# Feed forward of a transformer block: four tiles of each layer in a row, and a batch's output added two tiles later

## The reference

```
h = _layernorm(x, ln3_g, ln3_b)
p = h @ ff_w1 + ff_b1                       # 256 -> 2048
a, gate = (p[..., :D_FF], p[..., D_FF:])    # D_FF = 1024
h = a * jax.nn.gelu(gate, approximate=False) @ ff_w2 + ff_b2   # 1024 -> 256
return h + x
```

## Time and profile before

| what | value |
|---|---|
| time, median of 3 runs | 2804.77 us (2804.6 to 2804.89) |
| the profiled execution | 2804.19 us, its span 2802.4 us |
| PE / DVE / ACT / POOL busy over the span | 99% / 79% / 67% / 59% |
| TensorE's mean granted clock | 0.999 |
| feed forward, 2500 to 2600 us: PE / DVE / ACT / POOL | 100.00 / 55.82 / 42.25 / 51.14 us |
| one batch of the feed forward | 16.40 us, 144 matmuls |

### The profile page before, as it was taken

The page is one execution under the profiler, slowest core; times in us unless marked ns, Lnnn a source line. Parts: engine busy times, 40 slices in busy tenths (PEclk is TensorE's granted clock), DMA queues, the critical chain, the costliest instruction groups (busy, mean ns, idle before and its releaser), DMA issues.

```text
span 2802.4 us, 73115 instructions
## 1 busy us (share of the span) xinstructions
PE 2782.4 (99%) x25278; PEld 2488.9 (89%) x25278; DVE 2212.5 (79%) x3432; ACT 1885.2 (67%) x5979; POOL 1664.0 (59%) x1500
## 2 busy tenths in 40 slices
PE   8999999999999999999999999999999999999999
PEld 7888888888888888888888888888888899999999
DVE  7888888888888888888888888888888865555554
ACT  6776777777777777777777777777777754444443
POOL 5555555555555555776666666666666665555554
PEclk9999999999999999999999999999999999999999
DMA  6666666666666666677777777677767632222222
GB/s 160 150 162 165 162 161 158 161 156 155 150 150 153 156 157 153 152 182 177 180 181 176 177 181 170 165 169 171 172 169 168 156 101 87 75 75 85 83 75 65
DMA packets 355330, 413.34 MB, mean 147 GB/s; under 512 B 122016, under 2 KB 209440, under 8 KB 355232
## 3 DMA queue, kind: packets, MB, share of 16 engines
q1 hardware_dynamic: 345088, 395.29, 58.2%
q10 hardware_dynamic: 10144, 16.78, 1.6%
HBM read 94.52 MB, written 49.02 MB: 51 GB/s over the span
## 4 chain that ended last, share of the span: by engine, by line
PE 94%; POOL 2%; DVE 2%; issue 0%; ACT 0%; DMA 0%; SPq 0%; DVEq 0%; ACTq 0%; POOLq 0%
PE unit_ps L641 53%; PE unit_ps L666 15%; PE s_ps L653 14%; PE s_ps L641 12%; POOL probs L1385 1%; DVE blocks L1151 1%; DVE neg_max L1137 1%; POOL w_lo L1380 1%; ACT probs L936 0%; DVE qk L1163 0%; DMA pT<-blocks 0%; DVE w_lo L1097 0%; DVE hT L1132 0%; POOL x_rb L1372 0%; DMA x_ln<-in_x_dram 0%
## 5 line engine op out<-in xcount | busy, mean ns | idle before, releaser
L1385 POOL TENSOR_TENSOR probs<-probs,row_inv 128x1024 f32<-128x1024 f32 x512 | 971.5, 1897 | 827.6 <-DVE row_inv L1142 827.5
L936 ACT ACTIVATE probs<-s_ps,neg_max 128x256 f32<-128x256 f32 x2048 | 947.1, 483 | 467.9 <-DVE neg_max L1137 466.9
L1151 DVE STREAM_TRANSPOSE blocks<-probs 128x1024 f32<-128x1024 f32 x512 | 633.0, 1236 | 148.1 <-POOL probs L1385 147.5
L1137 DVE TENSOR_REDUCE neg_max<-s_ps 128x4 f32<-128x1024 f32 x512 | 612.4, 1196 | 12.7 <-PE s_ps L653 5.6
L641 PE MATMUL unit_ps<-hT_hi,w_hi 128*128 128x256 f32 x2048 | 580.0, 287 | 4.2 <-DVE hT_lo L1182 2.3
L641 PE MATMUL unit_ps<-hT_hi,w_lo 128*128 128x256 f32 x2048 | 554.9, 277 | 0.0
L641 PE MATMUL unit_ps<-hT_lo,w_hi 128*128 128x256 f32 x1792 | 497.4, 278 | 0.0
L666 PE MATMUL unit_ps<-pT,v_f 128*64 128x256 f32 x4096 | 456.4, 381 | 0.1
L936 ACT ACTIVATION_READ_ACCUMULATOR probs<-s_ps,neg_max 128x1 f32 x2048 | 437.9, 214 | 0.0
L653 PEld LDWEIGHTS s_ps<-qk 64*128 64x128 f32 x6144 | 375.2, 185 | 70.4 <-issue 53.3
L653 PE MATMUL s_ps<-qk 64*128 64x256 f32 x6144 | 427.1, 285 | 5.7 <-ACT probs L936 5.2
(11 more groups left out here) (81 smaller groups left out, 4917.3 us busy)
## 6 DMA issues: line engine op xcount, KB each, us to landing
pT<-blocks SPq DMA_DIRECT2D x1024, 256.0 KB, 4.5
rows_t_dram<-row_blocks SPq DMA_DIRECT2D x91, 256.0 KB, 2.4
rows_in<-rows_t_dram SPq DMA_DIRECT2D x91, 256.0 KB, 4.6
x_res<-in_x_dram SPq DMA_DIRECT2D x32, 256.0 KB, 3.1
x_sa_dram<-x_out SPq DMA_DIRECT2D x32, 256.0 KB, 2.2
x_ln<-x_sa_dram ACTq DMA_DIRECT2D x32, 256.0 KB, 4.4
ctx_in<-in_ctx_dram SPq DMA_DIRECT2D x32, 256.0 KB, 4.1
x_res<-x_sa_dram SPq DMA_DIRECT2D x32, 256.0 KB, 3.4
```

What stands on the lines that cost most here:

```text
L936: op = nc.scalar.activation(probs[:, m % 2, r, :].rearrange("p (j b c) -> p j b c", j=IT, c=BLK), scored.rearrange("p (j c b) -> p j b c", ...
L1137: nc.vector.tensor_reduce(neg_max[:, m % RING, :], s_ps[:, m % 2, :, :].rearrange("p h (i j) -> p (h i) j", j=S), AX_X, ALU.max, negate=Tr ...
L1151: nc.vector.transpose(blocks[:, n % 2, :, m % 2, :].rearrange("p b (j r c) -> p r j b c", j=IT, c=BLK), probs[:, m % 2, :, :].rearrange("p ...
L1385: nc.gpsimd.tensor_tensor(probs[:, m % 2, :, :], probs[:, m % 2, :, :], row_inv[:, m % RING, :].unsqueeze(2).broadcast_to([P, ROWS, S]), A ...
```

## The change

In a middle batch and in the last one TensorE now takes `hidden` 0 to 3, then the downs 4 to 7 of the batch before, then `hidden` 4 to 7, then its own downs 0 to 3. The first batch and the drain follow: the first does its downs 0 to 3 only (0 behind tile 5), the drain the downs 4 to 7. DVE adds the output of batch t-1 behind tile 3 rather than behind tile 1. Nothing is changed in the lists of ACT, POOL and SP.

```
                 if parts in (STEADY, LAST):
-                    for m in range(0, FT, 2):
+                    for m in range(FT // 2):
                         hidden(t, m, parity)
-                        hidden(t, m + 1, parity)
-                        for d in (m - 2, m - 1):
-                            if d >= 0:
-                                down(t, d)
-                            else:
-                                down(t - 1, d + FT)
+                    for m in range(FT // 2, FT):
+                        down(t - 1, m)
+                    for m in range(FT // 2, FT):
+                        hidden(t, m, parity)
+                    for m in range(FT // 2):
+                        down(t, m)
                     return
...
-                    if m < 2 and "prv" in parts:
-                        down(t - 1, m + FT - 2)
+                    if m < FT // 2 and "prv" in parts:
+                        down(t - 1, m + FT // 2)
...
-                        for d in {4: (0,), 5: (1,), 6: (2, 3), 7: (4, 5)}.get(m, ()):
+                        for d in {5: (0,), 6: (1,), 7: (2, 3)}.get(m, ()):
                             down(t, d)
...
-                    if m == 1 and "prv" in parts:
+                    if m == 3 and "prv" in parts:
                         dve.wait_ge(ff.xrb_done, t)
```

## The result

| | before | after |
|---|---|---|
| median, us | 2804.83 (2804.6 to 2806.04) | 2826.67 (2824.26 to 2827.98) |
| ratio, 95% interval | | 1.0076 [1.0064, 1.0089] |
| profiled execution; its span | 2804.19; 2802.4 | 2825.83; 2824.0 |
| busy in the span: PE, DVE, POOL | 2782.4, 2212.5, 1664.0 | 2789.8, 2188.0, 1674.4 |

A forecast was written before the change was run, and what follows sets the result against it. TensorE, busy 99% of the span, was taken as the bound. Late loads in SP's queue lengthen batches by 0.48 or 0.66 us; with batch 1 and the ends this sums to +16.45, forecast 2821 us, range 2802 to 2833.

The forecast's parts named there:

- Bound, pace: Feed forward: TensorE is full; two fewer returns from down to hidden save 0.04 us a batch, 16.36 if nothing waits.
- Cover of the addition on PE and DVE: Middle batches: addition done at 8.85 instead of 5.16, banks wanted only at 13.6, so the delay is free there.
- The chain behind it: SP's queue: store and loads move by 3.7 us, rows_lo ends late, next batch starts 0.48 (odd: 0.66) us later.
- The queue's delay: SP's queue: from the addition's end to L626 stays 2.35 us in even batches, 2.53 in odd ones.
- The sequencer's 0.45: Batch start on TensorE: 0.45 us taken between the wait for rows_lo and the first matmul; zero the other end.
- the small stall: Rival at the batch start: sequencer's 0.45 mostly hidden, 2808 us, covering 2803 to 2812 outside the forecast; chance 0.10.
- The block: POOL's remainder beside DVE's rows_lo: they exclude each other, rows_lo ends 0.54 behind it; without this, 2.7 us lower.
- Batches 1 and 2: First batches: late landings in batch 1 add 0.8 us to its odd 0.66; batch 2 loses the even 0.48.
- Start and end: Kernel's ends: returns saved in first and last two batches -0.1 us; covered wait for POOL at the end -0.65.
- The sum: Whole kernel: 16.4 for the batches, 0.8 for batch 1, -0.1 and -0.65 give +16.45 us.
- What would show it: Profile signs: PE 3 to 4 us below 100, clock 1.00, rows_lo waits 29 times, periods 16.9 and 17.1, shorter scaling.

The follow-up runs named there:

- both: The changed kernel with SP's loads of transposed rows and x_ln ahead of the wait for the addition, and POOL's residual add behind tile 7: 2803.5 us, 0.9995.
- pe_order_only: The changed kernel with the addition back behind tile 1 in DVE's list, TensorE's new order kept: 2822.44 us, 1.0063.
- loads_first: The changed kernel with SP's loads of transposed rows and x_ln ahead of the wait for the addition; load of x_res still behind the store: 2806.06 us, 1.0004.
- residual_last: The changed kernel with POOL's residual add moved from behind tile 3 to behind tile 7, after the remainders: 2817.93 us, 1.0046.
- both_old_order: The kernel before, old order kept, with SP's loads of rows and x_ln ahead of the addition's wait and POOL's residual add last: 2805.36 us, 1.0002.
- loads_first_old_order: The kernel before, old order kept, with only SP's loads of transposed rows and x_ln moved ahead of the wait for the addition: 2837.26 us, 1.0113.
- addition_only: The kernel before with only DVE's addition moved behind tile 3, TensorE in its old order: 2881.98 us, 1.0271.

## The prediction against the runs, step by step

**Bound, pace.** Right. Batches of 16.36 in both are the worked-out 0.04 less than 16.40.

**Cover of the addition on PE and DVE.** Right: pe_order_only and loads_first show that neither engine lost by it. The end of the addition was forecast at 8.85 of the batch and was 8.91.

**The chain behind it.** Medians of the 13 even and 13 odd batches from 3 to 28, in us from the batch's first matmul:

| | forecast even / odd | measured even / odd |
|---|---|---|
| L626 issued | 11.20 / 11.38 | 11.41 / 11.56 |
| L533 issued | 11.92 / 12.18 | 12.13 / 12.37 |
| x_rb starts | 13.90 / 14.08 | 14.22 / 14.37 |
| rows_lo starts | 15.61 / 15.87 | 15.77 / 16.22 |
| rows_lo done | 16.43 / 16.61 | 16.75 / 16.94 |
| next batch | 16.88 / 17.06 | 16.89 / 17.08 |

The periods came out within 0.02, and this was partly luck: two terms were off by about 0.3, in opposite directions.

- *The queue's delay was too small by 0.2.* Expected was that the interval from the addition to L626 stays. It grew from 2.35 / 2.53 to 2.50 / 2.65. In after L544 is issued 0.57 behind the store, where it was 1.0 to 1.1, and the store's landing releases L626 2.46 after its issue instead of 2.33. That the nearer load is the reason wasn't tested. x_res then takes 0.1 more as well (2.8 to its add, against 2.7), and x_ln in the odd batches: 3.05 from L533 to the statistics, against 2.9 (2.83 in the even ones).
- *The sequencer's 0.45 was wrong.* From rows_lo's end to the next matmul it is 0.13 in nearly all batches. What I had read in the earlier trace rows was a queue that runs ahead of a busy engine: the wait was over early and the matmul waited for its turn, so the interval was no latency. The row couldn't show one, since TensorE wasn't idle there, and rows_lo had ended 1.8 us before that batch began.

With the 0.13 and no other correction the sum would have been 16.56 and 16.74, and some 2812: slower still, but at the upper edge of the small stall. That rival named the right doubt about this step.

**The block.** Its mechanism was right, and its size was too small: worth 2.7 us in the forecast, 7 to 9 in the runs (residual_last). I had counted one remainder beside rows_lo; there are two, back to back, and three outcomes. If rows_lo starts well inside the first, it ends about 0.55 behind it (1.17 in the first lines shown, 2562.14 to 2563.31), and the second is held, so that the pair takes 1.88. If it starts some 0.1 before the first one's end it keeps its 0.69, and the pair takes 1.9 too (rows_lo of 2579.66 above). If the second gets in first, rows_lo has to wait for that one as well. That is batch 21, which took 17.76 (and batch 25, 17.66):

```profile
2647.03 1.42 POOL L1414 TENSOR_TENSOR pT<-probs,pT 128x256 fp32r<-128x256 f32 x2
2647.73 1.27 DVE L1213 TENSOR_TENSOR pT<-hT,pT 128x512 fp32r<-128x512 f32 x1
...
2649.13 0.50 PE L641 MATMUL s_ps<-pT,w_hi 128*128 128x256 f32 x2 [1.11 <-DVE pT L1213]
```

The pair keeps its 1.42, and rows_lo ends at 2649.00, 0.55 behind it. The Trainium skill (SBUF — State Buffer, Who interferes with whom) has the rule that one of the two is locked out while the other reads; by that rule the trace agrees, with up to 0.6 us as the loser's loss.

**Batches 1 and 2: the step that failed.** I had given batch 1 0.66 + 0.8, and batch 2 0.48. They cost 2.5 and 2.2 over 16.40, 2.8 us more together, over half of the 5.2 by which the sum was short. Batch 1 in after:

```profile
2296.74 0.40 SPq L620 DMA_DIRECT2D out_dram<-x_out  x1
...
2300.54 0.39 SPq L626 DMA_DIRECT2D x_res<-x_ca_dram  x1
...
2303.34 1.28 POOL L1372 TENSOR_TENSOR x_rb<-x_res,out_bias 128x512 f32<-128x512 f32 x1 [4.25 <-DMA x_res<-x_ca_dram]
2304.63 0.76 DVE L1108 BATCH_NORM_STATS2 bn<-x_ln 128x6 f32<-128x256 f32 x2 [2.36 <-DMA x_ln<-x_ca_dram]
2305.42 1.11 DVE L1213 TENSOR_TENSOR pT<-hT,pT 128x512 fp32r<-128x512 f32 x1
2306.66 0.50 PE L641 MATMUL s_ps<-pT,w_hi 128*128 128x256 f32 x2 [2.39 <-DVE pT L1213]
```

I had put the slow landing on L626, as in the earlier trace rows, where the store landed in time. Here it is the store that lands slowly, 3.6 us, and all that is behind it moves. The loads that followed were of usual length (2.7 and 3.0). And batch 2 pays for what TensorE's clock did afterwards. The window of 2306 to 2312:

```profile
2306.00:2312.00 6.00, 5.34 (x32) 5.34 (x33) 3.59 (x10) 2.06 (x5) 2.62 (x6) 0.72 0.00 0
```

After the wait of 2.4 us the granted clock was 0.72 over this stretch, a mixture of the full level (2.4 GHz) and the lower one (1.2 GHz): over 2308 to 2311 it was 0.50, and from 2307.8 to 2311.0 the matmuls came at 0.213 us and not at 0.1133. In the 5.34 us from its start batch 2 ran 32 matmuls, where the pace allows 47: 15 x 0.1133 = 1.7 of its 2.2 us. In pe_order_only, in which PE waited for 1.1 us there, the clock of this window stayed at 1.00; in residual_last, with the store landing after 3.9 us and a wait of 2.4 of PE, it was 0.72 again. The prediction had no term for the clock.

**Start and end.** Forecast -1.4 and +0.7, measured -1.0 and +0.9. The 48 matmuls without a break are there:

```profile
2815.10 5.77 PE L641 MATMUL unit_ps<-qk,pT 128*128 128x256 f32 x48
```

Without the tail of 0.16 these are 5.61, or 0.117 each and not 0.1133: 0.17 more. The first `hidden` of the feed forward starts up to 2.2 us apart in kernels whose attention is the same (2267.95 in before, 2268.46 in after, 2270.18 in both_old_order), so 0.4 there means nothing. Counted from that first matmul, batch 1 begins after 19.3 us where it was 20.8, close to the -1.4.

**The sum.** Forecast +16.45, measured +21.6 in the span. Batches 1 and 2: 2.8. The two batches in which POOL's second remainder came first: 2 x 0.6 = 1.2. The other 26 of batches 3 to 30: 0.5. Start and end: 0.6. Together 5.1.

**What would show it.** The clock at 1.00 in the middle, waits at all starts behind rows_lo (27 of PE, 2 more of its weight load), both DMA waits, periods in turn and the shorter scaling (0.74, was 2.12) all came. Not as forecast: the interval from the addition to L626, and PE's busy time, 2.3 us under 100 and not 3 to 4 (the count of matmuls shows the 3.6).

## What to carry to other kernels

Before an instruction that feeds a store is moved, list what stands behind that store in its queue, and who waits for the last of it; here the moved addition cost nothing on its own engine and 22 us through SP. Put loads that can go at once ahead of a store that must wait, and an add that needs a late load behind the work that others wait for, but do the two together: each alone can move the wait to another engine, as loads_first_old_order did. Don't read a latency from a wait that a busy engine covers.

## What the runs showed of the hardware

- Two back-to-back POOL instructions and one DVE instruction with two inputs: the one that comes first holds the other. DVE's 0.69 became up to 1.27, POOL's pair of 1.42 became 1.9, and the loser ended some 0.55 behind the winner. Whether DVE lost nothing or 0.6 was decided by less than 0.1 us of its start.
- In after the granted clock fell to its lower level after TensorE had waited for 2.4 us at the end of batch 1 (in residual_last too), and not after the waits of up to 1.1 us of the batches that followed. The length of one wait doesn't settle it: in addition_only TensorE waited 1.75 to 1.84 us in each batch, and the clock fell in six of them.
- A 256 KB store that usually lands in 2.3 us took 3.6 in batch 1, and 3.9 in residual_last. In after, a load of instructions fell beside it; in pe_order_only too, where the store took 2.4. Why it was slow stays open.
- From the end of the DVE instruction that TensorE stands waiting for to the first matmul: 0.13 us (after, batches 1 to 27).
